# A graph-attention kernel: where DVE loads tile numbers, where a tile's shares and next rows stand among the groups, when gelu's table is loaded, and how many tiles the tail takes

## The chip, the cores and the metric

The kernel runs on one core of a Trainium2 chip. The metric is the device time of one execution in microseconds (us).

## The reference

Two layers of graph attention over 3125 nodes (D = 128, 8 heads of 16) and 100000 edges, sorted by their destination node, plus one self loop for each node. The destinations are drawn as the integer part of 3125 u squared, with u uniform between 0 and 1, so early nodes have many more edges than late ones. What one layer computes, cut to what matters:

```
xn  = layernorm(x)                                  # ln1
xp  = xn + xn @ Wpos + bpos + deg * Wdeg + bdeg
q, k, v = xp @ Wq + bq, xp @ Wk + bk, xp @ Wv + bv
att = clip(sum_per_head(q[dst] * k[src]) / 4, -50, 50)
ex  = exp(att)                                      # normalised by its sum for each destination
aggr = segment_sum(ex * v[src], dst) / segment_sum(ex, dst)
x   = x + aggr @ Wo + bo
x   = x + gelu(layernorm(x) @ W1 + b1) @ W2 + b2    # hidden width 512
```

At the end out = layernorm(x_input + x).

## The kernel before

Nodes stand in 25 tiles of 128 (NT). Edges stand in 98 groups of 1024 (NG), each of 8 chunks of 128. For every group and layer:

- POOL gathers the rows k and v of the source nodes, one indirect DMA a chunk (L538), into one of four buffers kv. It starts on group g when the message product of group g - 4 is done.
- ACT makes hotT, the one-hot matrix of the group's destinations against one node tile (L666 dist, L669 hotT). PE multiplies it with q (L1257, 24 matmuls) and so spreads q over the edges in PSUM. A pair is one group with one tile; where a group crosses from one tile to the next it has two pairs, and there are 122 pairs a layer.
- DVE multiplies q with k (L1029 prod), sums over each head (L1032 dots), clips (L1034 to L1037 att). ACT takes the exponential (`weights`, L673 and L675). DVE makes the other one-hot (L950 hot), multiplies v with the exponential (L1055 msg), and PE sums messages and exponentials per node (L1271). DVE adds that sum into acc (L946, `evacuate`). The second pair of a crossing group is done in the group after it (`further_tiles`).

From group 48 on, each two groups (an even and an odd one) form a slot, 24 in all (FIRST_SLOT to SLOT_END, NSLOT), in which one finished node tile goes through the rest of the layer: share_out (L966 rsum, L968 ag, acc divided by its sum), transpose and Wo on PE, add_attention (L982 and two statistics), root on ACT (L612, L614), z1 (L987), transpose, W1 (L1228), gelu (L629), W2 (L1234, L1235), add_ffn (L993 in layer 0, L996 and L998 in layer 1), z2 (L1010), and in layer 0 the transpose and the product with the next layer's weights (L1245) and next_row (L1019), which SP then stores to the table that POOL gathers from in layer 1. The steps are spread over the slot's own two groups and the four after it: `slot`, `slot - 1` and `slot - 2` in `edge_group` and `pe_group` are the three tiles in flight.

Which tile a slot takes is data: DVE works out slot_tab (`slot_words_out`), by the rule that slot n may only take a tile that lies below the first tile of groups 47 + 2n and 48 + 2n, and that the tile number grows by one a slot at most. An engine that needs the number reads it with slot_tile:

```python
def slot_tile(eng, j):
    t = eng.value_load(slot_tab[0:1, bass.ds(j, 1)], min_val=0, max_val=NT - 2)
    return eng.snap(t.with_bounds(min_val=0, max_val=NT - 2))
```

It is a register load by the engine's sequencer (L371), with some arithmetic behind it. pair_words (L346) does the same for the first and last pair of each group. slot_tab[NSLOT] holds the first tile that the slots have not done, at most NT - TAIL (tail_start, L376); slots_less_tiles (L390) gives the running number of a later tile.

After group 97 the tail follows: the tiles from tail_start to NT - TAIL one after the other in a loop (`If(start < NT - TAIL)`, `Fori`), then the last TAIL tiles together, each step for all of them before the next step. In layer 0 POOL can begin layer 1's gathers only when the last row is stored.

The order of work on each engine is the order of the program; there is no planner. ACT's functions come in table sets: exp and ln in one, gelu in another. `log_and_exp()` loads the first (L638); the load for gelu is put before the first gelu by the compiler (L629 ACT_TABLE_LOAD).

## Time and profile before

| | us |
|---|---|
| median of 3 runs | 2221.33 (2219.34 to 2226.15) |
| the profiled execution | 2219.82 |
| its span, first to last instruction | 2217.9 |
| POOL busy | 1506.8 (68%) |
| PE busy | 1476.3 (67%) |
| DVE busy | 1472.5 (66%) |
| ACT busy | 925.3 (42%) |
| mean granted TensorE clock | 0.804 |

Busy is time in which an engine executes; a gap is idle time before an instruction, with what ended it: "issue" means that nothing but the engine's own sequencer was waited for. Register loads do not count as busy. Times in a timeline are from the start of the span. Group g of a layer is the g-th L1029 of that layer, counted from 0.

### The profile page before, as it was taken

The page shows a single profiled execution, that of the slowest core. Times are in us where ns is not written, and L with a number is a line of the kernel's source. Part 1 is how long each engine was busy: PE and PEld are TensorE (multiplying, and loading weights), DVE is VectorE, ACT ScalarE, POOL GpSimd, SP SyncE. Part 2 cuts the span into 40 slices and gives each one's busy share as a digit, 9 for nine tenths or more (in the row PEclk, how much of TensorE's full clock was granted, in tenths as well). Part 3 has the DMA queues.
Part 4 walks back from the last instruction along what each step waited for, and adds up shares of the span by engine and source line. Part 5 has one row for each costly group of instructions (what it writes and reads, how often), then busy time and mean ns, then how long its engine had stood idle before and what let it go on. Part 6 is the DMA issues. An engine that isn't in the chain of part 4 may idle for free.

```text
span 2217.9 us, 43957 instructions
## 1 busy us (share of the span) xinstructions
PE 1476.3 (67%) x11737; PEld 1314.0 (59%) x11738; DVE 1472.5 (66%) x2507; ACT 925.3 (42%) x1652; POOL 1506.8 (68%) x1584
## 2 busy tenths in 40 slices
PE   6745565566577787777764655656657777777776
PEld 5635554555566676666643554545546666666665
DVE  8786565665667677767757556565656767776665
ACT  3143232233246555556543222323324645464553
POOL 1557777777777777777407777777777777776650
PEclk8768777777778988889977667688788888888887
DMA  3345555545455555545315454545555555454430
GB/s 82 126 126 166 157 159 156 162 153 161 153 156 169 158 160 159 168 144 158 103 48 162 153 161 153 161 153 162 155 159 156 163 156 158 155 164 139 143 120 7
DMA packets 120462, 321.82 MB, mean 145 GB/s; under 512 B 31458, under 2 KB 43862, under 8 KB 120348
## 3 DMA queue, kind: packets, MB, share of 16 engines
q0 software_dynamic: 75072, 205.10, 30.8%
q1 hardware_dynamic: 44438, 113.89, 15.7%
q10 hardware_dynamic: 838, 1.60, 0.3%
q8 instruction: 37, 0.61, 0.1%
q14 instruction: 77, 0.63, 0.1%
HBM read 311.92 MB, written 8.55 MB: 144 GB/s over the span
## 4 chain that ended last, share of the span: by engine, by line
POOL 35%; issue 20%; PE 18%; DVE 15%; DVEq 6%; ACT 5%; DMA 1%; ACTq 1%; POOLq 0%; SPq 0%
POOL kv L538 35%; PE ps L1271 7%; PE ps L1257 4%; DVE dots L1032 2%; DVE prod L1029 2%; PE ps L1228 2%; DVEq L346 2%; DVE q_parts L801 2%; DVEq L371 1%; ACT L629 1%; ACT dist L666 1%; ACT hotT L669 1%; PE ps L1234 1%; DVE msg L1055 1%; DVE acc L946 1%
## 5 line engine op out<-in xcount | busy, mean ns | idle before, releaser
L538 POOL DMA_INDIRECT kv<-kv_tab,src_idx x1564 | 1482.1, 948 | 601.9 <-issue 470.0
L1271 PE MATMUL ps<-msg,hot 128*128 128x136 f32 x3904 | 667.1, 338 | 351.2 <-DVE acc L946 343.0
L1271 PEld LDWEIGHTS ps<-msg,hot 128*128 128x128 f32 x3904 | 619.7, 240 | 400.5 <-DVE msg L1055 220.7
L1257 PE MATMUL ps<-q_parts,hotT 128*128 x5856 | 505.2, 253 | 298.6 <-DVE prod L1029 173.4
L1257 PEld LDWEIGHTS ps<-q_parts,hotT 128*128 x5856 | 445.7, 114 | 359.5 <-issue 337.9
L1029 DVE TENSOR_TENSOR prod<-kv,ps 128x1024 f32<-128x1024 f32 x196 | 238.7, 1218 | 317.2 <-DMA kv<-kv_tab,src_idx 295.7
L950 DVE SCALAR_TENSOR_TENSOR hot<-dst_col,neg_base,ps 128x1024 f32<-128x1024 f32 x244 | 312.1, 1279 | 130.6 <-issue 106.3
L666 ACT ACTIVATE dist<-dst_rows,neg_node 128x1024 bf16<-128x1024 int32 x244 | 280.2, 1148 | 148.2 <-issue 133.8
L673 ACT ACTIVATE msg<-att 128x64 f32<-128x64 f32 x196 | 49.4, 252 | 603.3 <-DVE att L1037 601.8
L669 ACT ACTIVATE hotT<-dist 128x1024 bf16 x244 | 257.8, 1057 | 44.6 <-ACT dist L666 43.7
L1032 DVE TENSOR_REDUCE dots<-prod 128x64 f32<-128x1024 f32 x196 | 239.1, 1220 | 6.7
L1055 DVE TENSOR_TENSOR msg<-kv,ps 128x1024 f32<-128x1024 f32 x196 | 237.9, 1214 | 0.9 <-ACT ps L675 0.6
L608 ACT ACTIVATE agT<-ps 128x128 f32<-128x128 f32 x50 | 13.9, 278 | 222.3 <-PE ps L1214 222.3
L946 DVE TENSOR_TENSOR acc<-acc,ps 128x136 f32 x244 | 70.9, 291 | 48.3 <-PE ps L1271 43.1
L1228 PE MATMUL ps<-z1T,w1g 128*128 128x128 f32 x400 | 61.7, 302 | 30.0 <-issue 29.1
L1228 PEld LDWEIGHTS ps<-z1T,w1g 128*128 128x128 f32 x400 | 53.5, 207 | 35.2 <-issue 34.5
L1234 PE MATMUL ps<-w,hid_slot 128*128 128x128 f32 x400 | 61.0, 301 | 10.1 <-ACT hid_slot L629 9.9
L638 ACT ACT_TABLE_LOAD x52 | 66.7, 1283 | 0.9
L629 ACT ACT_TABLE_LOAD x50 | 64.2, 1283 | 0.9
L1234 PEld LDWEIGHTS ps<-w,hid_slot 128*128 128x128 f32 x400 | 54.8, 212 | 14.3 <-ACT hid_slot L629 14.1
L629 ACT ACTIVATE hid_slot<-ps,b1f 128x128 f32<-128x128 f32 x200 | 57.2, 368 | 4.6 <-PE ps L1228 3.9
L624 ACT ACTIVATE z1T<-ps 128x128 f32<-128x128 f32 x50 | 13.8, 276 | 101.1 <-PE ps L1223 101.1
(205 smaller groups left out, 1039.7 us busy)
## 6 DMA issues: line engine op xcount, KB each, us to landing
dst_rows<-in_dst SPq DMA_DIRECT2D x194, 512.0 KB, 4.0
kv<-kv_tab,src_idx POOLq DMA_INDIRECT x1564
kv_tab<-qkv SPq DMA_DIRECT2D x27, 128.0 KB
kv_tab<-qkv SPq DMA_DIRECT2D x3, 768.0 KB, 3.7
out<-z SPq DMA_DIRECT2D x25, 64.0 KB
dst_rows<-in_dst SPq DMA_DIRECT2D x2, 336.0 KB, 3.8
hot<-in_L_gnn_W SPq DMA_DIRECT2D x2, 256.0 KB
w<-in_L_gnn_W SPq DMA_DIRECT2D x2, 256.0 KB
```

Source lines behind the costliest of these rows:

```text
L538: pool.indirect_dma_start(kv[:, u, c, :], None, kv_tab[l][:, :], bass.IndirectOffsetOnAxis(ap=src_idx[:, c, at(g)], axis=0)).then_inc(kv_i ...
L629: last = nc.scalar.activation(hid[s][:, c * P:(c + 1) * P], banks["h"][c], ACT.Gelu, bias=b1f[:, l, c:c + 1])
L666: nc.scalar.activation(dist[:, :], dst_rows[:, r, :], ACT.Abs, bias=neg_node[:, at(t)]).then_inc(dist_done[l], 1)
L669: nc.scalar.activation(hotT[:, bass.ds(pr % 2, 1), :], dist[:, :], ACT.Relu, bias=1.0, scale=-1.0).then_inc(hotT_ready[l], 1)
L950: nc.vector.scalar_tensor_tensor(out=hot[:, u % 2, :, :], in0=dst_col[:, :, at(g)].broadcast_to([P, GC, P]), scalar=neg_base[:, at(t)], in ...
L1029: nc.vector.tensor_tensor(prod[:, :].rearrange("p (c d) -> p c d", d=D), kv[:, u, :, 0:D], qd.rearrange("p (c d) -> p c d", d=D), ALU.mult ...
L1032: nc.vector.tensor_reduce(dots[:, :], prod[:, :].rearrange("p (n d) -> p n d", d=HD), AX.X, ALU.add).then_inc(dot_done[l], 1)
L1055: nc.vector.tensor_tensor(half[:, :, 0:D].rearrange("p c (h d) -> p c h d", d=HD), kv[:, u, :, D:2 * D].rearrange("p c (h d) -> p c h d", ...
L1228: last = MM(banks["h"][c], w1g[:, l, c * P:(c + 1) * P], z1T[s], start=True, stop=True)
L1234: MM(banks["y"], hid[s][:, c * P:(c + 1) * P], w2[:, l, c, :], start=(c == 0), stop=False)
L1257: last = MM(qd[:, c * P:(c + 1) * P], hotT[:, bass.ds(pr % 2, 1), c * P:(c + 1) * P], q_parts[:, at(t), k * D:(k + 1) * D], start=first an ...
L1271: last = MM(agg, hot[:, u % 2, c, :], msg[:, u % 2, c, :], start=(c == 0), stop=(c == GC - 1))
```

## The change

Five edits. (1) DVE's slot_tile loads, which stood right before the steps that use them, stand behind the issue of the product L1029: `current` in every group of an opening slot, and `passed` and `finished` too in the odd one. (2) share_out moves from before the one-hot L950 to behind it, with a wait that the tile's last sum has been added; the wait for ag itself goes behind the message product, and no longer counts up numbers_read. next_row moves from the end of the even group to the middle of the following odd one (behind add_attention), with SP's store for it one group later in layer 0; on PE project_next goes before hidden. (3) ACT copies z2T before z1T. (4) ACT loads gelu's table explicitly before it waits for h, and computes gelu before it copies agT, both in the slots and (the load) in the tail. (5) TAIL is 2, not 3. At the end of a layer DVE adds the last sum before next_row and reads the tail's numbers before it waits; PE does sum_further before project_next.

```diff
-TAIL = 3
+TAIL = 2
...
-                    k = (g - 8) // 2
-                    if g % 2 == 0 and FIRST_SLOT <= k < SLOT_END:
+                    k, step = divmod(g - (9 if l < L - 1 else 8), 2)
+                    if step == 0 and FIRST_SLOT <= k < SLOT_END:
...
+                def gelu_only():
+                    nc.scalar.preload_act_table_set("gelu_and_others")
+
...
+                    if even and not_before(slot, 2):
+                        copy_z2T(slot - 2, 0, in_slot)
                     if even and not_before(slot, 1):
                         copy_z1T(slot - 1, 0, in_slot)
-                    if even and not_before(slot, 2):
-                        copy_z2T(slot - 2, 0, in_slot)
...
+                    if even and not_before(slot, 1):
+                        gelu_only()
+                        gelu(slot - 1, 0, in_slot)
                     if even and opens(slot):
                         copy_agT(slot, 0, in_slot)
                     if even and not_before(slot, 1):
-                        gelu(slot - 1, 0, in_slot)
                         log_and_exp()
...
+                    if slot is not None and opens(slot):
+                        current = slot_tile(dve, slot)
+                    if odd and not_before(slot, 1):
+                        passed = slot_tile(dve, slot - 1)
+                    if odd and not_before(slot, 2):
+                        finished = slot_tile(dve, slot - 2)
                     dve.wait_ge(prod_done[l], g + 1)
...
-                    if even and opens(slot):
-                        share_out(slot_tile(dve, slot), slot, 0)
-                        wait_for_number(dve, ag_done[l], slot + 1)
                     if odd and not_before(slot, 1):
-                        passed = slot_tile(dve, slot - 1)
                         add_ffn(passed, slot - 1, 0, in_slot)
                     if odd and opens(slot):
-                        add_attention(slot_tile(dve, slot), slot, 0, in_slot)
+                        add_attention(current, slot, 0, in_slot)
+                    if odd and not_before(slot, 2):
+                        next_row(finished, slot - 2, 0, in_slot)
...
                     one_hot(u, g, tile_of(dve, a, shift))
+                    if even and opens(slot):
+                        dve.wait_ge(evac_done[l], a + 1)
+                        share_out(current, slot, 0)
                     if ahead:
                         word(d + 1)
...
+                    if even and opens(slot):
+                        dve.wait_ge(ag_done[l], slot + 1)
                     if not opened:
                         evacuate(a, last_shift)
...
-                    if even and not_before(slot, 2):
-                        next_row(slot_tile(dve, slot - 2), slot - 2, 0, in_slot)
...
-                next_row(slot_tile(dve, NSLOT - 1), NSLOT - 1, 0, in_slot)
                 end, shift = word(NG - 1)
                 further_tiles(NG - 1, NG - 1, word(NG - 2)[0], end, shift)
+                finished = slot_tile(dve, NSLOT - 1)
+                start = tail_start(dve)
+                n = tail_number(dve)
                 evacuate(end, shift)
+                next_row(finished, NSLOT - 1, 0, in_slot)
...
+                    if even and not_before(slot, 2):
+                        project_next(slot - 2, 0, in_slot)
                     if even and not_before(slot, 1):
                         hidden(slot - 1, 0, in_slot)
                     if even and opens(slot):
                         transpose_ag(slot, 0, in_slot)
-                    if even and not_before(slot, 2):
-                        project_next(slot - 2, 0, in_slot)
...
+                sum_further(1, word(NG - 2)[0], word(NG - 1)[0])
                 project_next(NSLOT - 1, 0, in_slot)
-                sum_further(1, word(NG - 2)[0], word(NG - 1)[0])
```

## Rows read from the trace of the kernel before

**Rows 1.** The page: chain by engine, and the costliest group (last: idle before)

```profile
POOL 35%; issue 20%; PE 18%; DVE 15%; DVEq 6%; ACT 5%; DMA 1%; ACTq 1%; POOLq 0%; SPq 0%
...
L538 POOL DMA_INDIRECT kv<-kv_tab,src_idx x1564 | 1482.1, 948 | 601.9 <-issue 470.0
```

**Rows 2.** POOL's waits, whole span: us in all, times, longest

```profile
POOL kv L538 <- DVE msg L1055: 45.2, 19, 13.6
```

**Rows 3.** Timeline of POOL: start, us, instruction [idle before <- releaser]

```profile
584.17 0.94 POOL L538 DMA_INDIRECT kv<-kv_tab,src_idx  x1 [0.30 <-issue]
...
864.35 0.95 POOL L538 DMA_INDIRECT kv<-kv_tab,src_idx  x1 [0.30 <-issue]
...
1640.32 0.95 POOL L538 DMA_INDIRECT kv<-kv_tab,src_idx  x1 [0.30 <-issue]
```

**Rows 4.** Timelines of POOL and DVE, plain group 38, layer 0

```profile
492.90 0.95 POOL L538 DMA_INDIRECT kv<-kv_tab,src_idx  x1 [0.30 <-issue]
...
495.81 1.22 DVE L1029 TENSOR_TENSOR prod<-kv,ps 128x1024 f32<-128x1024 f32 x1 [3.81 <-DMA kv<-kv_tab,src_idx]
...
499.40 1.28 DVE L950 SCALAR_TENSOR_TENSOR hot<-dst_col,neg_base,ps 128x1024 f32<-128x1024 f32 x1 [0.28 <-issue]
```

**Rows 5.** Windows: us, busy of PE, PEld, DVE, ACT, POOL, clock

```profile
604.80:1114.90 510.10, 395.10 (x3279) 348.70 (x3280) 367.67 (x678) 284.39 (x535) 361.03 (x382) 0.87 0.49 151
...
1661.00:2176.40 515.40, 384.26 (x3205) 346.10 (x3205) 361.63 (x678) 280.03 (x510) 360.88 (x382) 0.85 0.48 146
```

**Rows 6.** Line L371, DVE's sequencer: ns min/median/max

```profile
L371 DVEq FUSED_REGOPS  x240: 53/190/210, 599.3 to 2190.8; - x120
L371 DVEq TENSOR_LOAD <-slot_tab x192: 298/305/441, 598.9 to 2190.5; - x192
L371 DVEq SEQ_ASSERT  x192: 23/23/33, 599.5 to 2191.1; - x192
```

**Rows 7.** Timeline of DVE, even group 70 of layer 0

```profile
831.52 0.20 DVE L966 RECIPROCAL rsum<-acc 128x8 f32 x1 [0.65 <-issue]
...
832.81 1.28 DVE L950 SCALAR_TENSOR_TENSOR hot<-dst_col,neg_base,ps 128x1024 f32<-128x1024 f32 x1 [0.66 <-DVE ag L968]
```

**Rows 8.** DVE's waits in the slots' stage, layer 0; last, layer 1

```profile
DVE qkv L1019 <- PE ps L1245: 19.3, 13, 2.5
DVE acc L946 <- PE ps L1271: 15.5, 10, 2.2
DVE x L982 <- issue: 14.6, 23, 1.0
DVE rsum L966 <- issue: 14.4, 23, 0.7
...
DVE x L993 <- issue: 7.2, 13, 0.6
...
DVE prod L1029 <- issue: 4.0, 3, 2.1
...
DVE x L996 <- PE ps L1235: 33.1, 21, 3.9
```

**Rows 9.** Timeline of DVE, group 97 and tail, layers 0 and 1

```profile
1114.94 1.22 DVE L1029 TENSOR_TENSOR prod<-kv,ps 128x1024 f32<-128x1024 f32 x1
...
1131.99 0.20 DVE L966 RECIPROCAL rsum<-acc 128x8 f32<-128x8 f32 x1 [1.58 <-issue]
...
1138.90 0.32 DVE L987 TENSOR_SCALAR z<-x,spot 128x128 f32<-128x128 f32 x1
...
1146.77 0.29 DVE L993 TENSOR_TENSOR x<-x,ps 128x128 f32<-128x128 f32 x1 [6.84 <-PE ps L1235]
...
1155.74 0.61 DVE L1019 SCALAR_TENSOR_TENSOR qkv<-degw,degn,ps 128x384 f32<-128x384 f32 x1 [0.46 <-PE ps L1245]
...
2176.46 1.21 DVE L1029 TENSOR_TENSOR prod<-kv,ps 128x1024 f32<-128x1024 f32 x1
...
2183.00 0.29 DVE L996 TENSOR_TENSOR x<-x,ps 128x128 f32<-128x128 f32 x1 [3.45 <-PE ps L1235]
```

**Rows 10.** Timeline of ACT, even group 88 of layer 1

```profile
2089.66 0.28 ACT L608 ACTIVATE agT<-ps 128x128 f32<-128x128 f32 x1 [4.26 <-PE ps L1214]
2089.95 1.28 ACT L629 ACT_TABLE_LOAD   x1
```

More of the change, by code:

```diff
@@ L727, in _ @@
                         scale_x2(n, 0)
+                        gelu_only()
                         copy_z1T(n, 0, in_slot)
@@ L737, in _ @@
                     scale_x2(n + f, f)
+                gelu_only()
                 for f in range(TAIL):
@@ L1084, in _ @@
                     edge_group(g % SLOTS, g // SLOTS, g, word, g, ahead=g < NG - 1, slot=NSLOT)
-                next_row(slot_tile(dve, NSLOT - 1), NSLOT - 1, 0, in_slot)
                 end, shift = word(NG - 1)
                 further_tiles(NG - 1, NG - 1, word(NG - 2)[0], end, shift)
+                finished = slot_tile(dve, NSLOT - 1)
+                start = tail_start(dve)
+                n = tail_number(dve)
                 evacuate(end, shift)
+                next_row(finished, NSLOT - 1, 0, in_slot)
                 settle(dve)
                 dve.wait_ge(evac_done[l], end + 2)
-                start = tail_start(dve)
                 with dve.If(start < NT - TAIL):
                     with dve.Fori(start, NT - TAIL) as t:
-                        n = early_number(dve, t)
-                        share_out(t, n, 0)
-                        add_attention(t, n, 0, in_slot)
-                        normalise_x2(n, 0)
-                        add_ffn(t, n, 0, in_slot)
-                        normalise_x3(t, n, 0)
-                        next_row(t, n, 0, in_slot)
-                n = tail_number(dve)
+                        m = early_number(dve, t)
+                        share_out(t, m, 0)
+                        add_attention(t, m, 0, in_slot)
+                        normalise_x2(m, 0)
+                        add_ffn(t, m, 0, in_slot)
+                        normalise_x3(t, m, 0)
+                        next_row(t, m, 0, in_slot)
                 tail = [(NT - TAIL + f, n + f, f) for f in range(TAIL)]
```

## The prediction

> **What bounds the kernel now.** I read the page first. Its costliest group is the gather on POOL [rows 1]: 1564 indirect DMAs, each 0.95 us of POOL and then 0.30 us of "issue". That is 1.25 us for a chunk and 10.0 us for a group of eight. The chain that ended last also names POOL first, though with 35% only [rows 1], so something else bounds part of the time. POOL's own waits say how much: it waited for the product L1055 (a kv buffer that comes free) for 45.2 us in all, 13.6 of them once at the start [rows 2].
>
> Then the timeline of POOL, for its pace. From group 48 to group 76 of layer 0 it issues without a wait: (864.35 - 584.17) / 28 = 10.006 us a group [rows 3]. In a plain group DVE needs less: it sits idle for 3.81 us until the gather lands, 2.0 us after POOL's last issue (492.90 + 0.95 to 495.81) [rows 4]. So groups 0 to 47 are POOL's, and nothing that DVE saves there counts.
>
> From group 48 on, every two groups also carry one node tile (a "slot"). Two windows show this stage, 48 groups each: 510.1 us in layer 0, which is 10.63 a group, and 515.4 us in layer 1, 10.74 a group [rows 5]. Both are above POOL's 10.006. DVE is busy for 367.7 and 361.6 us of them, so 142 and 154 us are idle between its instructions, nearly all of it not for the gather. DVE falls behind until POOL has to wait for it. The stage is bound by DVE's serial stream, with PE and ACT in its gaps. The reader is to see that POOL's pace is a floor under any gain here.
>
> **The floor.** If POOL alone set the pace, layer 0's group 97 would have its first issue at 584.17 + 49 x 10.006 = 1074.5, its sixth and last issue ended 7.2 later and data 2.0 after that: its product L1029 at 1083.6 instead of 1114.94 [rows 3, 4, 9], 31.3 us earlier. Layer 1: 1640.32 + 490.3 + 9.2 = 2139.8 instead of 2176.46, 36.7 earlier, and the 3.45 us wait for y in that last group [rows 9] may go too: 40.1.
>
> **The change part by part, layer 0's stage.**
> Tile numbers. A load with its arithmetic holds DVE's sequencer for 0.305 + 0.190 + 0.023 us and three steps of about 0.034: 0.62 [rows 6]. Today three of four such loads stand behind an instruction of 0.2 us, and each shows as a gap, 0.65 before L966 for one [rows 7]. In the stage the gaps are 14.6 us before L982, 14.4 before L966, and before L993 13 of 0.55 each [rows 8], the ten others being put down to PE though the load fills them too: 23 x 0.55 = 12.6. That is 41.6 us in 69 gaps. Behind the 1.22 us product the loads run while the engine works, and a wait of about 0.1 remains for each: 34.7 saved.
> Share later. L950 now comes 0.66 us after ag, in a plain group 0.28 after att [rows 4, 7]: 0.38 x 23 = 8.7 saved.
> Next row later. Its wait for PE is 19.3 us [rows 8]. A group later the product is long there, and about 0.15 x 23 = 3.5 us of address work stays: 15.8 saved.
> Sum 59.2. Against it: the odd group has three loads under one product, 3 x 0.62 = 1.86 against 1.22 us, so 0.64 or somewhat more (address arithmetic) comes before L1032. I take 0.7 x 24 = 17. If none of the load ran under the product it would be 45, if the gap before L1032 is only the excess 15. And in the even group the word of the next group is loaded behind ag (0.29 us) and no longer behind L950 (1.28): about 0.4 to 0.6 is exposed, 12. Net 30: 480 us for 48 groups, 10.0 a group. That is POOL's pace.
> The sequencer's load is what speaks against this edit most. The Trainium skill, "DMA: Bandwidth & Descriptors", section "Latency and other measured facts", gives a register load a floor of about 600 ns. The trace has 305 ns, so the measurement decides. By the page's figure three loads would hold 2.7 us and not 1.9, and the two costs together would be about 58 and not 29: nothing would be left of the stage's gain.
>
> **Layer 1's stage.** There is no next row to compute. Gaps before L966 and L982 are like those above, 46 of them: about 25 saved. The load after L946 goes: 4. L950: 8.7. The largest is new: DVE waits 33.1 us for y (L996 on PE L1235) [rows 8]. y needs gelu, and gelu stands on ACT behind the copy of agT and a table load of 1.28 us [rows 10]. With gelu's table loaded during the wait for h and the copy behind gelu, h's values come 1.5 to 2 us earlier in each of 21 such waits. I take 25 of 33. Together 62, less the same 29: 482 us, 10.05 a group. The same edit lets the one-hots of the next group start up to 1.5 us earlier, which may shorten the 15.5 us that L946 waits for PE in this stage of layer 0 [rows 8]. I count it as nothing, with 0 and 15 as bounds.
> The table load: hidden wholly it gives 1.28 us, not hidden 0. The Trainium skill, "ScalarE: Activation LUTs", section "What ACT_TABLE_LOAD costs", puts 1.38 us of drain beside each load, 2.66 in all. By the trace the first gelu starts at the load's end (2089.95 + 1.28, no idle time between), so 1.28 is the price here.
>
> A demand equal to the floor does not reach the floor: groups with a second tile pair (18 of them from 49 to 95) and DVE's loop turn every 12 groups come in lumps, and every other group carries a pair near the end. I leave 5 us of lag at group 97 in layer 0 and 7 in layer 1. Layer 0 gives 31.3 - 5 = 26, layer 1 gives 40.1 - 7 = 33.
>
> **The tail.** Here I expect the change to cost. Slot 23 runs in group 94, which begins at edge 96256. By the reference's draw that edge's node is 3125 x 0.9626 squared = 2895, in tile 22. So tile 22 is unfinished, no slot can take it, and the slot table ends at 22. With three tiles in the tail 22 equals NT - TAIL and the loop between is skipped. With two, NT - TAIL is 23, so tile 22 goes through that loop alone, one serial chain, and then come the two.
> The batch of three in layer 0 lasts from 1131.99 to about 1156.4 (L1019 at 1155.74 plus 0.61) [rows 9], 24.4 us. Its stages go tile by tile: 6.9 us to the first z1, 7.9 to the first y, 9.6 to the end of the last next row. In them the first tile waits for the others. Each further tile costs an estimated 1.45 us of x2 additions, 1.6 of PE's products, 1.5 of y's additions, 1.1 of next rows and 0.4 of small things. So two tiles take 6.0 less: 18.4.
> One tile alone has the same three stretches without the others: 6.9 - 2.2 = 4.7 (two further x2 additions, of which the root overlaps 0.7), 7.9 - 1.75 = 6.1 (PE's further hidden products), and 9.6 - 4.5 = 5.1. That is 15.9, and about 0.5 for the loop. Layer 0 is then 16.4 + 18.4 - 24.4 = +10.4 us. Layer 1 has no z2T and next row (13.6 with the loop) and saves only 5.0: +8.6. The number's load moves ahead of the wait, and the 1.58 us gap before L966 [rows 9] shrinks by 1.2 in layer 0 and 0.6 in layer 1. Net +9.2 and +8.0. Bounds for each layer: +6 if the chain's table load is hidden and PE gets the slots' granted clock of 0.87 [rows 5], +12 if the new loop costs two gaps of the size of the longest before L1029, 2.1 us [rows 8].
>
> **Sum.** -26 - 33 + 9.2 + 8.0 = -41.8 us (1.2 and 0.6 of it the earlier load). The profiled execution took 2219.82 us (span 2217.9), which gives 2178. The median shown, 2221.33, is 1.5 higher: 2179 us.
>
> **Rivals.**
> POOL paces all: the shorter ACT chain takes L946's waits away and no lag is left. -31.3 - 40.1 + 17.2 = -54: 2167. For it speaks that DVE's demand is counted with all PE waits kept; against it the lumps. Chance 0.17.
> PE and ACT are next: a group with two pairs needs two one-hots on ACT, 48 matmuls and a further sum in a row, and L946 waits on that already. The gaps saved on DVE then reappear as waits for PE, and the stage runs at about 10.35 and 10.4: -13 - 19 + 17 = -15: 2206. For it: 15.5 us of such waits [rows 8] with DVE slow. Chance 0.19.
> Slower: the serial tile of the tail. Its price is 17.2 us, while the stage's gain is a balance of 59 against 29. It decides where both stages together give under 17 us, which is 0.18 a group. At a gain of 10 the time is 2228, at none 2238. Chance 0.10. By the page's figure for a register load, quoted above, the stages would give about 4 us together and the time would be 2235; the 0.305 us of [rows 6] are why it gets no more than this chance.
> The tail is shorter and no serial tile runs, because the slot table reaches 23: -59 - 6.0 - 4.9 - 1.8 = -72: 2149. The node of edge 96256 speaks against it: 0.03.
> The gain and the tail cancel within 0.3%: 0.05. My forecast: 0.46.
>
> A measurement of this kernel tells about 0.3%, 6.7 us, from no change. Faster 0.85, within 0.3% 0.05, slower 0.10. The range 2162 to 2207 leaves out the slower, the cancelled and the short tail (0.18).
>
> **What would show it.** POOL's waits for L1055 inside the stage nearly gone. Windows of 48 groups at 481 to 490 us. Gaps before L966, L993 and L982 near 0.1. A new gap of about 0.7 before the reduction in odd groups. L1019 without a wait. The wait for y in layer 1 under 10 us. The tails longer by 8 to 10 us each, with three share-outs, the first alone. The forecast is wrong if the reduction's gap is above 1.5 us, if L946's wait for PE grows, or if the tail shows no single tile.

## The result, and the profile after

The changed kernel took 2187.47 us (median of 4 runs, 2184.3 to 2192.76) against 2220.34 us of the kernel before beside it: a ratio of 0.985, 95% interval 0.9823 to 0.9877. It is faster by 1.5%; forecast were 1.9% and 2179 us. The profiled execution is the longest of its runs, 2192.76 us with a span of 2190.9, so 27.1 us under the 2219.82 of before. Two executions of the second set below ran at a lower granted clock than all others (2300.0 us at 0.60 and 4627.01 us at 0.29); the medians of that set are without them.

The page first: the chain that ended last now runs through POOL for 58% of the span, 35% before [rows 1].

```profile
POOL 58%; issue 21%; PE 8%; DVE 6%; ACT 2%; DMA 2%; DVEq 1%; ACTq 0%; POOLq 0%; SPq 0%
```

POOL's waits over the whole span, which answer [rows 2]: 15.7 us are left, 13.6 of them the one at the start.

```profile
POOL kv L538 <- DVE msg L1069: 15.7, 8, 13.6
```

The stage with slots in windows, columns as in [rows 5]. It takes 483.65 and 484.20 us, 10.08 and 10.09 a group, where POOL's pace is 10.006.

```profile
608.25:1091.90 483.65, 368.95 (x3274) 324.58 (x3273) 365.36 (x677) 282.88 (x531) 361.22 (x382) 0.93 0.52 159
1653.60:2137.80 484.20, 367.51 (x3205) 331.74 (x3203) 359.74 (x677) 280.12 (x511) 361.50 (x382) 0.89 0.51 156
```

DVE's waits inside these two windows (us, times, longest), layer 0 and then layer 1, against [rows 8]. What DVE now waits for most is the gather.

```profile
DVE prod L1036 <- DMA kv<-kv_tab,src_idx: 37.6, 24, 3.0
...
DVE dots L1045 <- DVE prod L1036: 12.2, 18, 0.8
DVE acc L953 <- PE ps L1286: 11.2, 7, 3.1
DVE msg L1069 <- issue: 10.8, 23, 0.7
...
DVE prod L1036 <- DMA kv<-kv_tab,src_idx: 29.1, 19, 3.6
...
DVE x L1003 <- PE ps L1250: 7.8, 9, 2.4
```

The timeline of DVE in an odd and the following even group of layer 0. The odd group waits 0.67 us between the product and the reduction L1045: that is what three loads last longer than the product over them. The additions and the next row behind it show no gap. In the even group the shares L973 follow the one-hot at once, where [rows 7] had 0.65 before them; the message product L1069 has 0.50 before it, the load of the next group's pair words.

```profile
829.57 1.22 DVE L1036 TENSOR_TENSOR prod<-kv,ps 128x1024 f32<-128x1024 f32 x1 [1.94 <-DMA kv<-kv_tab,src_idx]
831.47 1.22 DVE L1045 TENSOR_REDUCE dots<-prod 128x64 f32<-128x1024 f32 x1 [0.67 <-DVE prod L1036]
...
835.21 0.61 DVE L1026 SCALAR_TENSOR_TENSOR qkv<-degw,degn,ps 128x384 f32 x1
...
848.18 0.20 DVE L973 RECIPROCAL rsum<-acc 128x8 f32 x1
...
849.30 1.22 DVE L1069 TENSOR_TENSOR msg<-kv,ps 128x1024 f32<-128x1024 f32 x1 [0.50 <-issue]
```

Then the tail of layer 0, DVE's timeline, against [rows 9]. One tile goes through alone, from its shares at 1110.20 to the shares of the batch at 1128.07: 17.9 us. The batch of two lasts until 1148.99, 20.9 us.

```profile
1110.20 0.20 DVE L973 RECIPROCAL rsum<-acc 128x8 f32 x1 [0.48 <-issue]
...
1114.98 0.35 DVE L994 TENSOR_SCALAR z<-x,spot 128x128 f32<-128x128 f32 x1 [0.60 <-ACT spot L614]
1122.81 0.29 DVE L1000 TENSOR_TENSOR x<-x,ps 128x128 f32 x1 [7.49 <-PE ps L1250]
...
1128.07 0.20 DVE L973 RECIPROCAL rsum<-acc 128x8 f32<-128x8 f32 x1
...
1141.83 0.29 DVE L1000 TENSOR_TENSOR x<-x,ps 128x128 f32<-128x128 f32 x1 [7.43 <-PE ps L1250]
...
1148.38 0.61 DVE L1026 SCALAR_TENSOR_TENSOR qkv<-degw,degn,ps 128x384 f32<-128x384 f32 x1 [0.55 <-PE ps L1260]
```

The two profiled executions, cut at the same places (us):

| part | before | after | difference | forecast |
|---|---|---|---|---|
| start to POOL's first gather | 89.61 | 93.06 | +3.5 | 0 |
| first gather to product of group 97, layer 0 | 1025.33 | 998.83 | -26.5 | -26 |
| that product to the end of its message product | 8.71 | 9.12 | +0.4 | 0 |
| from there to layer 1's first gather (the tail) | 35.35 | 50.95 | +15.6 | +9.2 |
| first gather to product of group 97, layer 1 | 1017.46 | 985.85 | -31.6 | -29.7 |
| that product to the end of its message product | 12.06 | 11.18 | -0.9 | -3.4 |
| tail of layer 1 | 29.43 | 41.93 | +12.5 | +8.0 |

The first line is scatter: eight kernels with the same start, on two other chips, had that gather between 87.1 and 92.2. The prediction gave layer 1 as 33 in one piece; 3.45 of it is a wait for y that stands behind group 97's product, so it is forecast in the line below.

### The profile page after: what moved, and what is told of

It is laid out like the page before. It is cut to its first block, busy times and chain, and to the rows that moved or that the text cites. A ratio compares the mean times of both kernels' runs of the same rounds, so it can differ in the third digit from the quotient of the medians.

```text
span 2190.9 us, 44032 instructions
## 1 busy us (share of the span) xinstructions
PE 1446.9 (66%) x11737; PEld 1284.3 (59%) x11738; DVE 1467.4 (67%) x2507; ACT 927.6 (42%) x1656; POOL 1507.2 (69%) x1584
## 3 DMA queue, kind: packets, MB, share of 16 engines
q1 hardware_dynamic: 44438, 113.89, 15.6%
## 4 chain that ended last, share of the span: by engine, by line
POOL 58%; issue 21%; PE 8%; DVE 6%; ACT 2%; DMA 2%; DVEq 1%; ACTq 0%; POOLq 0%; SPq 0%
POOL kv L538 58%; PE ps L1286 3%; DVE q_parts L808 2%; PE ps L1272 1%; DMA kv<-kv_tab,src_idx 1%; PE ps L1243 1%; DMA x<-in_x 1%; DVE prod L1036 1%; ACT dist L669 1%; PE ps L1249 1%; DVE dots L1045 1%; PE ps L1260 1%; ACT hotT L672 1%; DVEq L346 0%; DVE msg L1069 0%
## 5 line engine op out<-in xcount | busy, mean ns | idle before, releaser
L1286 PEld LDWEIGHTS ps<-msg,hot 128*128 128x128 f32 x3904 | 613.3, 238 | 387.4 <-DVE msg L1069 214.7
L1272 PE MATMUL ps<-q_parts,hotT 128*128 x5856 | 482.6, 245 | 289.3 <-DVE prod L1036 177.8
L1272 PEld LDWEIGHTS ps<-q_parts,hotT 128*128 x5856 | 422.7, 110 | 352.2 <-issue 329.8
L1045 DVE TENSOR_REDUCE dots<-prod 128x64 f32<-128x1024 f32 x196 | 239.1, 1220 | 32.0 <-DVE prod L1036 23.1
L1069 DVE TENSOR_TENSOR msg<-kv,ps 128x1024 f32<-128x1024 f32 x196 | 238.4, 1217 | 25.2 <-issue 22.1
L1243 PE MATMUL ps<-z1T,w1g 128*128 128x128 f32 x416 | 64.9, 305 | 18.8 <-issue 15.3
L1243 PEld LDWEIGHTS ps<-z1T,w1g 128*128 128x128 f32 x416 | 59.5, 214 | 29.6 <-issue 19.6
L521 POOL TENSOR_TENSOR hot<-hot,ident 128x128 f32<-128x128 f32 x2 | 21.6, 10796 | 47.3 <-DMA msg<-in_L_gnn_b 47.3
L612 ACT ACTIVATE spot<-spot,eps_col 128x1 f32<-128x1 f32 x108 | 31.1, 288 | 51.6 <-DVE spot L985 51.4
```

The costliest lines, as they stand in the source:

```text
L1045: nc.vector.tensor_reduce(dots[:, :], prod[:, :].rearrange("p (n d) -> p n d", d=HD), AX.X, ALU.add).then_inc(dot_done[l], 1)
L1069: nc.vector.tensor_tensor(half[:, :, 0:D].rearrange("p c (h d) -> p c h d", d=HD), kv[:, u, :, D:2 * D].rearrange("p c (h d) -> p c h d", ...
L1243: last = MM(banks["h"][c], w1g[:, l, c * P:(c + 1) * P], z1T[s], start=True, stop=True)
L1272: last = MM(qd[:, c * P:(c + 1) * P], hotT[:, bass.ds(pr % 2, 1), c * P:(c + 1) * P], q_parts[:, at(t), k * D:(k + 1) * D], start=first an ...
L1286: last = MM(agg, hot[:, u % 2, c, :], msg[:, u % 2, c, :], start=(c == 0), stop=(c == GC - 1))
```

## The experiments

**First set: the tail.** Four kernels, on a chip on which the kernel before took 3355.99 us (more on that at the end); ratios are to that. The tail is measured from the end of group 97's message product. Neither the kernel before nor the changed one left a trace on this chip, so tails are compared with those of the table above, from other chips.

The change with three tail tiles:

```diff
-TAIL = 2
+TAIL = 3
```

> The changed kernel with TAIL = 3 again and nothing else. Theory A (the serial tile of the tail is what the change overpaid): from the last message product to POOL's restart the changed kernel takes 50.9 us in layer 0 where the one before took 35.4, and 41.9 against 29.4 in layer 1. With three tiles together both come back to within 3 us of before: 24 to 28 us faster than the changed kernel, about 2162 us, ratio to before 0.973 to 0.976. Theory B (the forecast's 17 us for the serial tile was right and the 11 us missing lie in the groups): 17 us faster than the changed kernel, about 2170. Theory C (how many tiles are left for the tail does not matter): 2187.

Measured: 3290.52 us, ratio 0.9796 (0.9738 to 0.9855). Tails of 32.9 and 31.0 us, within 3 us of before's 35.35 and 29.43, as theory A has it.

The kernel before with two tail tiles:

```diff
-TAIL = 3
+TAIL = 2
```

> The kernel before with TAIL = 2 and nothing else. Theory A: one tile goes through the loop alone in both layers, plus the gelu table load of 1.28 us in its chain: 26 to 30 us slower than before, about 2248 us. Theory B: 17 to 20 us slower, about 2239. Theory C: 2220, no change.

Measured: 3377.44 us, ratio 1.005 (1.0021 to 1.008), slower by 21.4 us; the interval, 7 to 27 us, holds both A's lower end and B. Tails of 50.2 and 41.9 us, 15 and 12.5 above before's in the table, as in the changed kernel. So the longer tails come with TAIL, and do not need the new order of work.

The changed kernel, and the same with TAIL = 3, with PE kept at work in the tail:

```diff
+                def awake():
+                    for _ in range(8):
+                        MM(ps[:, 7, 0:P], zeros[:, :], zeros[:, :], start=True, stop=True, skip_group_check=True)
...
                         for part in (transpose_ag, project_out, transpose_z1, hidden, project_ffn, transpose_z2, project_next):
+                            awake()
                             part(n, 0, in_slot)
```

> The changed kernel with 8 small bf16 matmuls of zeros into an unused PSUM bank before each of the seven steps of PE in the tail, for the serial tile and for the last two. Their results are not used. Theory A1 (the tail is long because TensorE's granted clock is 0.50 for most of it: 30.7 us of layer 0's tail in the changed kernel, 13.7 then 6.8 at full clock before): PE's hidden products of the serial tile take nearer to 1.2 than 2.08 us, and the tails shrink by 2 to 5 us each: 2178 to 2184 us. Theory A2 (the chain of steps alone sets the length, and the clock is not moved by so little work): the extra matmuls, 0.4 to 0.9 us before each of 14 steps where PE is not yet idle, cost up to 5 us: 2187 to 2193.

> TAIL = 3 with the same 8 small matmuls before each of the seven steps of PE in the tail. Theory A1: 1 to 4 us faster than TAIL = 3 without them, 2158 to 2161. Theory A2: 0 to 3 us slower, 2162 to 2165.

Measured: 3312.88 us, 0.9875 (0.9818 to 0.9933), tails 47.0 and 41.8 with two tail tiles; and 3291.83 us, 0.98 (0.9736 to 0.9864), tails 32.1 and 32.0 with three. With intervals this wide the times tell nothing of the clock; it was tried once more in the third set.

**Second set: what carries the stage with slots.** Four kernels with three tail tiles on one chip, before 2224.34 us. "48 groups" below is the time from the product of group 49 to that of group 97, layer 0 and layer 1; it is 509.2 and 514.5 before, 482.6 and 482.7 in the changed kernel (the windows of [rows 5] begin 1 us earlier).

> The changed kernel with three tiles left for the tail, as before, and all else changed; once more beside the three kernels that follow. If the third tail tile costs what the tails of the first set measured (-15 to -18 us in layer 0, -11 to -12.5 in layer 1), and the stage with slots stays at the gathers' pace, it ends 26 to 30 us under the changed kernel's 2187: 2157 to 2161 us, 0.971 to 0.973 of before. The forecast's terms for the tail (+17 us together) would put it at 2170, 0.977.

Measured: 2161.87 us, 0.9742 (0.971 to 0.9774). 48 groups: 484.8 and 484.6. Tails 35.2 and 30.5, so 15.8 and 11.5 less than with two tail tiles. Between the medians lie 25.6 us, on two chips whose kernels before differ by 4.0.

Loads late again:

```diff
-                    if slot is not None and opens(slot):
-                        current = slot_tile(dve, slot)
-                    if odd and not_before(slot, 1):
-                        passed = slot_tile(dve, slot - 1)
-                    if odd and not_before(slot, 2):
-                        finished = slot_tile(dve, slot - 2)
                     dve.wait_ge(prod_done[l], g + 1)
...
+                    if even and opens(slot):
+                        current = slot_tile(dve, slot)
                     if odd and not_before(slot, 1):
+                        passed = slot_tile(dve, slot - 1)
                         add_ffn(passed, slot - 1, 0, in_slot)
...
-                        add_attention(current, slot, 0, in_slot)
+                        add_attention(slot_tile(dve, slot), slot, 0, in_slot)
...
-                        next_row(finished, slot - 2, 0, in_slot)
+                        next_row(slot_tile(dve, slot - 2), slot - 2, 0, in_slot)
```

> Three tail tiles, and VectorE's loads of tile numbers back behind the dots, where the kernel before has them; the rest of the change stays. Each load stands open with its checks again, about 0.5 us, three in an odd group and one in an even one: about +0.9 us a group, 43 us a layer. Theory, that the gathers set the pace of the stage: VectorE waited 37.6 and 29.1 us for them in the changed kernel, so that only what goes beyond comes out, and what stands open at the layer's last group: +5 to +20 us over the two layers on the kernel with three tail tiles, and VectorE's waits for the gathers nearly gone. Rival, that the loads carry the whole gain of the stage: +50 us or more, with POOL waiting for VectorE's messages as before.

Measured: 2212.76 us, 0.9948 (0.9927 to 0.9969): +50.9 us, the rival's number. 48 groups: 511.4 and 501.8. DVE's waits in layer 0 between the two products, first with early loads, then with late ones:

```profile
DVE prod L1036 <- DMA kv<-kv_tab,src_idx: 29.5, 17, 2.9
DVE acc L953 <- PE ps L1286: 16.6, 11, 2.7
...
DVE x L1000 <- PE ps L1250: 10.1, 13, 3.1
```

```profile
DVE hot L957 <- issue: 29.5, 25, 2.7
DVE x L1000 <- PE ps L1247: 29.4, 22, 2.6
DVE qkv L1026 <- issue: 16.9, 22, 1.1
DVE x L989 <- issue: 13.6, 23, 0.6
...
DVE prod L1036 <- DMA kv<-kv_tab,src_idx: 6.2, 4, 2.5
```

The loads open again in front of L989, L1026 and the one-hot, and the wait for y rises too, by 19.3 us; the load that now stands in front of L1000 accounts for an estimated 13 of them (22 times 0.59). The waits for the gathers did give way, from 29.5 to 6.2, but they covered only about half of the new gaps: 26.6 and 17.2 us came out. Nearly all that is left of them in layer 0 (5.4 us) lies in groups 51 to 53, and from group 58 on DVE never waits for a gather and falls behind POOL. What came out of layer 0 has two parts. Group 97's product starts 23.2 us after POOL's last issue, where it was 8.8 with early loads: 14.4 us. And POOL itself was held up, which the rival names: from group 85 on it waited 12.5 us for the message product, and its last issue came 12.8 us later after its first. In layer 1 the lag grew by 15.3 us, to 23.7, and POOL was held up for 4.2. The theory that POOL's pace absorbs the loads gave at most +20 us and falls.

Gelu late again:

```diff
                     if even and not_before(slot, 1):
-                        gelu_only()
-                        gelu(slot - 1, 0, in_slot)
                     if even and opens(slot):
                         copy_agT(slot, 0, in_slot)
                     if even and not_before(slot, 1):
+                        gelu(slot - 1, 0, in_slot)
                         log_and_exp()
```

> Three tail tiles, and gelu with its table back behind the copy of the share-outs; the rest of the change stays. The waits of VectorE for the layer 1 y product return: 33.1 us in 21 before against 7.8 in 9, so +25 us of VectorE's time in layer 1. Theory, that the gathers set the pace: VectorE's waits for the gathers in layer 1 (29.1 us) take them in, and the time rises by 0 to 8 us. Rival, that the early table is worth what its wait was: +25 us. Layer 0 is the same in both within 4 us.

(The explicit load in the tail is gone too.) Measured: 2195.2 us, 0.9879 (0.9846 to 0.9911): +33.3 us, and not in layer 1 alone. 48 groups: 508.1 and 499.3, so +23.3 and +14.7. The waits of layer 0:

```profile
DVE x L996 <- PE ps L1246: 35.3, 20, 4.4
DVE acc L949 <- PE ps L1282: 22.9, 11, 3.3
DVE prod L1032 <- DMA kv<-kv_tab,src_idx: 18.8, 11, 3.4
```

The wait for y is 35.3 us, against 10.1 with gelu early, and 28.4 in layer 1 against 10.4. In layer 1 that is the wait of before (33.1) coming back. In layer 0 it was small before (5.4 in ten, [rows 8] has the others as the load), and y is not made later than then: its product ends 12.7 us after the even group's product, against 12.8 in the kernel before (means of 22 slots), and agT is copied 8.6 us after it against 8.3, although the shares stand later. What moved is DVE. It comes to y 11.7 us after that product and not 13.3, since neither the next row nor a load stands in front of it any more. With the loads early but the shares, the next row and gelu in their old places (the last kernel below) the wait for y in layer 0 was 1.6 us. This points to the next row: its later place is what needs the early gelu. It is not shown by a run, since none moves the next row alone.

Fewer loads (the odd group keeps the even group's register, layer 1 loads no `finished`):

```diff
-                    if slot is not None and opens(slot):
-                        current = slot_tile(dve, slot)
+                    if even and opens(slot):
+                        held["current"] = slot_tile(dve, slot)
+                    current = held["current"]
...
-                    if odd and not_before(slot, 2):
+                    if odd and not_before(slot, 2) and l < L - 1:
                         finished = slot_tile(dve, slot - 2)
```

> Three tail tiles, and fewer loads: the odd group takes the number of its own tile from the even group's register, and layer 1, which has no next row, loads none for it. The odd group's gap of 0.67 us before the dots goes, 24 times a layer: -16 us of VectorE's time a layer. Theory, that the gathers set the pace: they give 0 to -6 us in all, and VectorE's waits for the gathers grow by about 16 us a layer. Rival, that VectorE still sets the pace: -25 to -32 us.

Measured: 2163.19 us, 0.9747 (0.9717 to 0.9776), 1.3 us above and no difference. 48 groups: 484.8 and 481.0. The gap before the reduction fell from 10.9 to 1.9 us in layer 0. The wait for y rose from 10.1 to 19.2 and the gathers' waits from 29.5 to 36.1, while the wait for the sum fell from 16.6 to 10.6:

```profile
DVE prod L1038 <- DMA kv<-kv_tab,src_idx: 36.1, 21, 3.0
DVE x L1000 <- PE ps L1253: 19.2, 14, 3.2
...
DVE dots L1048 <- DVE prod L1038: 1.9, 6, 0.4
```

At POOL's pace this gap less on DVE is worth nothing; in layer 0 not only the waits for the gathers take it in but those for PE too. The late loads, some 50 us of gaps more in layer 0, cost about half of themselves. The changed order stands near that corner.

**Third set: the other parts, and the clock.** One chip, before 2220.12 us.

> Three tail tiles, and the shares again before the one-hot L957, as in the kernel before; all else changed. It puts 0.38 us before the one-hot 23 times a layer, 8.7 us, but starts each tile's chain on PE and ACT 1.3 us earlier. Theory, from the two kernels with late loads and late gelu, in which about half of what VectorE lost came out in the stage: +4 to +9 us over the two layers on three tail tiles (2162). Rival, that the earlier chain takes as much from the waits for PE as the gap costs: 0 within 3 us.

```diff
+                    if even and opens(slot):
+                        share_out(current, slot, 0)
+                        wait_for_number(dve, ag_done[l], slot + 1)
                     if odd and not_before(slot, 1):
                         add_ffn(passed, slot - 1, 0, in_slot)
```

(and taken away behind the one-hot). Measured: 2162.75 us, 0.9735 (0.9708 to 0.9761), 0.9 us from the kernel with late shares, which is the rival's number; 48 groups 487.4 and 483.9, +2.6 and -0.7. The rival's reason is not borne out: in layer 0 the waits for y and for the sum did not fall (14.8 and 17.8 us, 10.1 and 16.6 with late shares). What evened it out is the word of the next group: the one-hot waits 11.4 us for ag again, but the 10.9 us before the message product are gone, since the word loads behind the long one-hot. Where the shares stand matters little once gelu is early.

> Three tail tiles, and the next row, its product on PE and its copy on ACT again in the even group, one group earlier, in their old order; all else changed. Only layer 0 computes next rows. The wait of the next row for PE, 19.3 us in 13 before, returns, and about 3.5 us of address work with it. Theory, that half to two thirds of it comes out: +10 to +17 us, all of it in layer 0. Rival, that the waits for the gathers take it in: 0 to +4 us. In both layer 1 stays within 3 us.

```diff
-                    if odd and not_before(slot, 2):
+                    if even and not_before(slot, 2):
                         finished = slot_tile(dve, slot - 2)
...
-                    if odd and not_before(slot, 2):
-                        next_row(finished, slot - 2, 0, in_slot)
...
                         normalise_x2(slot, 0)
+                    if even and not_before(slot, 2):
+                        next_row(finished, slot - 2, 0, in_slot)
```

(with project_next behind transpose_ag on PE, z1T's copy before z2T's on ACT, and SP's store a group earlier). Measured: 2155.35 us (2154.6 to 2157.39), 0.9706 (0.968 to 0.9733), while the kernel with early shares beside it took 2161.71 to 2166.6. It is the fastest kernel of this case, and both theories had the wrong sign. 48 groups: 480.0 and 483.2. Layer 0's waits:

```profile
DVE prod L1036 <- DMA kv<-kv_tab,src_idx: 24.1, 17, 2.6
DVE qkv L1026 <- PE ps L1260: 22.7, 17, 3.7
...
DVE acc L953 <- PE ps L1286: 9.6, 8, 2.1
```

The next row's wait did return, 22.7 us. But the waits for y (10.1) fell to 0.2 us, those for the sum from 16.6 to 9.6, and the gap before the reduction from 10.9 to 3.7, as the three loads are now spread two and two. These, with 5.4 us less of gathers, are 29.5 us; against them stand the 22.7 and smaller gaps, and the window is 4.8 us shorter. y's product is not made earlier (it ends 11.8 us after the even group's product, 11.9 with the late next row); DVE comes to it 0.65 us later, since it has waited for the next row before. Group 97's product follows POOL's last issue by 3.9 us here and by 8.8 with the late next row, and the tail of layer 0 is 2.1 us shorter. The edit also undoes the change's part (3), the order of ACT's copies; which of its pieces carries the gain is not shown.

> The changed kernel with eight more matmuls of 128 columns on zeros ahead of each step of the tail on PE, into a PSUM bank that the tail leaves free, so that TensorE is not idle while it waits. The stages are the same. Theory, that the tails ran over their forecast (by 6.4 and 4.5 us) because TensorE was granted 0.50: the tails get shorter by 4 to 8 us together, 2180 to 2184 us. Rival, that the granted clock of the tail has little hold on its time, or that the added matmuls stand before the real ones: within 2 us of the changed kernel, 2187.

The edit is that of the first set, with two tail tiles. Measured: 2181.83 us, 0.9825 (0.9798 to 0.9852), against 0.985 (0.9823 to 0.9877) of the changed kernel: -5.6 us between the medians, with intervals that overlap. Tails of 47.8 and 37.6 instead of 50.95 and 41.9, 7.4 us less together. Not all of that is the edit's: 2.2 us of it lie in layer 1 before the first share, nearly all in PE's last sum, which is over before the first of the added matmuls runs. The changed kernel, and this one:

```profile
2151.50 3.97 PE L1286 MATMUL ps<-msg,hot 128*128 128x136 f32 x16 [0.79 <-DVE acc L953]
```

```profile
2142.20 2.09 PE L1286 MATMUL ps<-msg,hot 128*128 128x136 f32 x16 [0.79 <-DVE acc L953]
2144.32 0.62 PE L1342 MATMUL ps<-zeros 128*128 128x128 bf16 x8
```

The other 5.2 us lie behind them: 0.5 and 1.65 in the lone tile, 2.6 and 0.45 in the batch of two.

> The kernel before with one part of the change alone: VectorE loads its tile numbers behind the long product, two in an even group and two in an odd one. Two loads of 0.62 us fit under one product of 1.22 us, so 34.7 us go in layer 0 and about 29 in layer 1. Theory, that the parts add up and the gathers' pace is the floor: the windows of 48 groups fall from 510 and 515 to about 485 and 490, -50 us, 2171. Rival, that what the loads free turns into waits for PE (the next row's, the y product's, the sum's), as nearly the whole gain of the stage went when either the loads or gelu were put back: -10 to -20 us, 2200 to 2210, with POOL still waiting for the message product.

```diff
+                    if slot is not None and opens(slot):
+                        current = slot_tile(dve, slot)
+                    if odd and not_before(slot, 1):
+                        passed = slot_tile(dve, slot - 1)
+                    if even and not_before(slot, 2):
+                        finished = slot_tile(dve, slot - 2)
                     dve.wait_ge(prod_done[l], g + 1)
```

(and these numbers used where the kernel before loads them). Measured: 2190.87 us, 0.9869 (0.984 to 0.9897), -29.3 us, between the two theories. 48 groups: 498.1 and 499.1. Layer 0's waits, against [rows 8]:

```profile
DVE qkv L1019 <- PE ps L1250: 26.7, 18, 3.2
DVE acc L946 <- PE ps L1276: 24.6, 13, 3.4
...
DVE prod L1029 <- DMA kv<-kv_tab,src_idx: 12.3, 8, 3.2
...
DVE msg L1060 <- ACT ps L675: 6.2, 5, 1.4
```

This kernel has three tail tiles, as before. Nearly all of the 41.6 us of gaps that the prediction counts went, and 11.0 came out in the stage (15.4 in layer 1; 4.8 of the profiled execution's gain lie in the tails). The next row's wait grew by 7.4 us (19.3 to 26.7), the sum's by 9.1 (15.5 to 24.6), and waits for the exponential rose to 6.2 from 0.2: PE and ACT are asked sooner and are not done. POOL is not held up any more from group 48 on; DVE's product of group 97 still follows its last issue by 22.2 us, and that lag is what remains. So the expectation's sign of the rival, POOL still waiting, did not show. Three moved loads alone bring nearly what the whole change brought with its longer tail (29.3 and 32.9 us).

## Why the prediction was right, and where it was off

**The stage reaches POOL's pace: shown.** 483.65 and 484.20 us lie in the forecast 481 to 490. POOL's waits inside the stage are gone, and group 97's product comes 26.5 and 31.6 us earlier. Forecast were 26 and 29.7 (33 less the 3.45 of y's wait behind that product, which did not go: 2.18 us of it stayed). The kernel with three tail tiles took 2161.9 us; the forecast without its tail term is 2179 - 17 = 2162, and against the kernel before beside it the gain is 62.5 us where the forecast has 59.

**The single gaps: as forecast, but for one.** 0.67 before the reduction (0.7), 0.47 before L1069 (0.4 to 0.6), y's wait in layer 1 at 7.8 us (under 10), L1026 without a wait in the stage, no gap before L973 and 0.4 us before L989. Before L1000, where about 0.1 each was forecast, 5.7 us in ten were left in layer 0, now waits for PE. The sum's wait for PE fell, from 15.5 to 11.2 us and from 15.0 to 11.8 in layer 1; counting it as nothing was a little too low. The register load is priced right: put back in front of L989, it opened 13.6 us in 23 gaps, 0.59 each. The Trainium skill's 600 ns for the load alone ("DMA: Bandwidth & Descriptors", section "Latency and other measured facts") does not agree: the load took 0.30 us here too, and load, arithmetic and checks together took about that floor.

**DVE's demand: over-estimated, and the floor hid it.** Forecast were 10.0 and 10.05 us a group. An estimate from the waits is lower: without those for gathers it was (483.65 - 37.6) / 48 = 9.29, and (484.20 - 29.1) / 48 = 9.48. That did no harm to the time, since POOL's pace is the floor. The lags of 5 and 7 us at group 97 had no row behind them; its product followed POOL's last issue by 6.4 and 6.6 us, so by 4.4 and 4.6 beyond the 2.0 that the data takes. That the stage's total came out so closely is in part luck: a wrong demand and a wrong term for the next row could both move without the time following.

**Adding up gaps as if each stood alone: right for the sum, wrong for the parts.** The terms (loads 34.7, shares 8.7, next row 15.8, y 25) were worked out one by one. Alone, the loads brought 11.0 us in layer 0. Taken out of the whole, they cost 26.6 there, and gelu 23.3, although gelu is not among layer 0's terms at all. The parts need each other: a wait for PE fills much of what a load leaves, unless its result is made earlier or asked for later.

**"Next row later ... 15.8" failed.** With all else changed, the late next row costs 4.8 us in the stage of layer 0, and 6.5 to 7.4 us between the medians. It saves its own wait, but puts a third load under one product, and DVE reaches y sooner and waits for it (10.1 us against 0.2) and waits longer for the sum (16.6 against 9.6).

**The tail: the mechanism right, the size off.** A single tile ran alone, as forecast from the edges' draw. The term is mis-sized, +9.2 and +8.0 against +15.6 and +12.5, both above the +6 to +12 given as bounds; that is 10.9 of the 14.7 us between forecast and profiled execution (3.5 are the start). The tails piece by piece (us, and the granted clock), forecasts by the prediction's terms:

| piece | forecast, layers 0 and 1 | measured | clock | over |
|---|---|---|---|---|
| end of message product to first share | 7.1, 6.0 | 9.2, 8.2 | 0.65, 0.61 | 2.1, 2.2 |
| the lone tile | 16.4, 13.6 | 17.9, 14.6 | 0.52, 0.55 | 1.5, 1.0 |
| the batch of two and what follows | 21.0, 17.8 | 23.9, 19.1 | 0.64, 0.68 | 2.9, 1.3 |

In the kernel before the first piece had 0.91 and 0.92, and the batch of three 0.69 and 0.68. So the lone tile itself is the smallest part of the miss. The first piece is not its doing at all, as it lies before it: it took 8.7 and 6.1 us in the kernel with three tail tiles too, at 0.59 and 0.50. It holds PE's last sums, for one of which DVE waited 4.20 us. In layer 1 the changed kernel and the one with the added matmuls do the same work in it, 8.2 us at 0.61 and 6.0 at 0.88. What sets the clock there was not tried out. The stretch from z1 to y is where the other two pieces ran over in layer 0: 7.8 us in the lone tile (forecast 6.1) and 8.5 in the batch of two (6.3). PE's timeline in the lone tile, and then in the batch of three before:

```profile
1116.58 2.08 PE L1243 MATMUL ps<-z1T,w1g 128*128 128x128 f32 x8 [0.73 <-ACT z1T L624]
1119.89 2.08 PE L1249 MATMUL ps<-w,hid_slot 128*128 128x128 f32 x8 [1.23 <-ACT hid_slot L629]
1121.89 0.79 PE L1250 MATMUL ps<-b_row,ones 1*128 1x128 f32 x2
```

```profile
1141.97 3.45 PE L1228 MATMUL ps<-kv,w1g 128*128 128x128 f32 x16
1145.26 1.06 PE L1234 MATMUL ps<-w,hid_slot 128*128 128x128 f32 x8
1146.25 0.48 PE L1235 MATMUL ps<-b_row,ones 1*128 1x128 f32 x2
```

Behind three tiles' hidden products in a row the second product ran at 1.06 + 0.48 us. Alone, with waits of 0.73 and 1.23 us for ACT between, it took 2.08 + 0.79. The windows give the granted clock of the two: 0.52 in the lone tile, its lower level (1.2 GHz) nearly throughout, and 0.69 in the batch of three. I had priced PE's work in every piece as in the kernel before; that its clock could be another stood only in the lower bound, as a better one. With more matmuls on zeros between the steps the same product was

```profile
1116.48 1.64 PE L1249 MATMUL ps<-w,hid_slot 128*128 128x128 f32 x8 [0.38 <-ACT hid_slot L629]
1118.05 0.48 PE L1250 MATMUL ps<-b_row,ones 1*128 1x128 f32 x2
```

and 5.2 of the 10.9 us came back in the pieces that have the added matmuls, where the clock rose to 0.62 and 0.74 in the lone tile and to 0.90 and 0.76 in the batch. On the first set's chip the tails were only 3.9 and 0.2 us shorter than the changed kernel's, which ran elsewhere. So the clock is shown, by one pair of traces, as part of the overrun. That it is all of it is not shown: the added matmuls stand in PE's way themselves, and times alone did not tell the two kernels apart. The Trainium skill, "TensorE: Matmul & The Clock Gate", section "Part 1: The HAM clock gate (the "warmup" mystery)", says that the clock follows how busy PE has been, and drops to half when it idles; by that rule, which I did not weigh, the trace agrees.

**The rivals.** "POOL paces all" came true for layer 0's stage once the next row was early again (480.0 us, where 48 x 10.006 is 480.3), not in the change as made. "PE and ACT are next" did not decide the change, but it is what the kernel with early loads alone ran into: 498.1 and 499.1 us are 10.38 and 10.40 a group, where that rival says 10.35 and 10.4. "The slot table reaches 23" is refuted by the lone tile.

## What to carry to other kernels

Ahead of an engine with a fixed pace, look for the corner: gaps taken away beyond it are worth nothing, gaps added in number cost at once (here about half of themselves), and slack early in a stage does not pay for demand late in it. On a serial engine that shares a chain with others, a gap taken away mostly turns into a wait for the next engine, unless the order of that one changes too. So price the parts of an edit together, and try each of them removed: the shorter TAIL was forecast as a loss and was a larger one, and the later next row was a loss hidden in a gain. And when work moves, ask what granted clock PE had in the rows that price it, and whether it will have it in the new place; here the tail's prices came from rows at 0.91 and 0.69, and it ran at 0.65, 0.52 and 0.64.

## What the runs showed of the hardware

The chip of the first set took 3355.99 us for the kernel before, half as long again as the others. POOL's instruction was the same there, 948 ns, but PE stopped within runs of matmuls for no wait that the profile shows. PE's waits over the span in the kernel with three tail tiles, on that chip and on the second:

```profile
PE ps L1272 <- issue: 365.0, 305, 22.6
PE ps L1286 <- issue: 231.4, 221, 4.3
```

```profile
PE ps L1272 <- issue: 11.8, 27, 1.0
...
PE ps L1286 <- issue: 3.0, 2, 1.8
```

POOL there waited 1144.9 us for DVE's message product. DVE in turn waited before its product: 183.7 us are put down to PE, and 871.1 to no engine of the core by name. Whether PE's sequencer got its instructions too slowly, or was held by something else that the profile does not record, stays open. The Trainium skill, "Runtime: NRT & Kernel Launch", section "Instruction fetch mechanics", says that the sequencer fetches its instructions itself by DMA and that this is mostly hidden; no run here shows whether it was late on that chip. The gain of the change with three tail tiles was 65.5 us there (the interval allows 49 to 88) and 62.5 on the second chip, so no dependence on it is shown.
